# Row sums of the squared queries as plain float32 matmuls, one head per strip of 32 array columns

## What is computed

```python
def rmsnorm(x, g, eps=EPS):
    var = jnp.mean(jnp.square(x), axis=-1, keepdims=True)
    return x * jax.lax.rsqrt(var + eps) * g
...
q = (hidden_states @ Wq).reshape(B, Sq, H, D)      # 16 heads of 128
q = rmsnorm(q, gq)
k = rmsnorm(k, gk)
scores = jnp.einsum('bqhd,bkhd->bhqk', q, k) * scale
attn = jax.nn.softmax(scores, axis=-1)
```

## Time and profile before

| | us |
|---|---|
| median of 3 runs | 1967.53 |
| lowest, highest | 1967.52, 1968.19 |
| span of the profiled execution | 1966.3 |

### The profile page before, as it was taken

The page is one execution under the profiler, slowest core; times in us unless marked ns, Lnnn a source line. Parts: engine busy times, 40 slices in busy tenths (PEclk is TensorE's granted clock), DMA queues, the critical chain, the costliest instruction groups (busy, mean ns, idle before and its releaser), DMA issues.

```text
span 1966.3 us, 33608 instructions
## 1 busy us (share of the span) xinstructions
PE 1946.3 (99%) x11232; PEld 1857.1 (94%) x11232; DVE 1598.0 (81%) x2995; ACT 1008.8 (51%) x2338; POOL 1141.3 (58%) x1272
## 2 busy tenths in 40 slices
PE   8999999999999999999999999999999999999999
PEld 7899899999999999999999999988999999999999
DVE  8878887787887787887778887888888888888875
ACT  5655555555555555555555543444444444444442
POOL 7765655423434333444333335788888888888871
PEclk9999999999999999999999999999999999999999
DMA  6444443423333323233223324211111111111101
GB/s 207 141 127 160 146 151 107 139 92 99 127 109 96 124 101 116 100 119 118 94 91 115 118 94 115 66 33 44 33 33 33 33 33 33 33 33 33 33 1 68
DMA packets 93514, 174.54 MB, mean 89 GB/s; under 512 B 13264, under 2 KB 49760, under 8 KB 91296
## 3 DMA queue, kind: packets, MB, share of 16 engines
q1 hardware_dynamic: 93344, 172.39, 26.7%
HBM read 139.00 MB, written 33.36 MB: 88 GB/s over the span
## 4 chain that ended last, share of the span: by engine, by line
PE 88%; DVE 5%; POOL 3%; issue 2%; ACT 1%; DMA 1%; SPq 0%; DVEq 0%; ACTq 0%; POOLq 0%
PE psum L429 43%; PE psum L819 19%; PE psum L460 6%; PE psum L493 4%; PE psum L516 4%; PE psum L501 4%; PE psum L522 3%; PE psum L517 3%; PE psum L591 1%; PE psum L532 1%; DVE g L1509 0%; DVE ysum L1542 0%; DVE g L1504 0%; DMA xb<-in_x 0%; DVE work L1381 0%
## 5 line engine op out<-in xcount | busy, mean ns | idle before, releaser
L927 ACT ACTIVATE work<-psum,stats,q_rstd 100x361 f32<-100x361 f32 x256 | 163.8, 651 | 166.6 <-DVE stats L1372 166.6
L1271 DVE TENSOR_TENSOR kaT_lo<-psum,kaT_hi 128x488 fp32r<-128x488 f32 (+2 forms) x384 | 213.9, 613 | 41.3 <-ACT kaT_hi L867 41.2
L429 PE MATMUL psum<-wk,ctxT_hi 128*122 128x512 f32 x768 | 241.0, 395 | 0.0
L2043 POOL TENSOR_TENSOR inter_lo<-g,inter_hi 128x400 fp32r<-128x400 f32 x127 | 143.2, 1133 | 125.9 <-ACT inter_hi L867 125.0
L867 ACT CAST kaT_hi<-psum 128x488 fp32r<-128x488 f32 (+2 forms) x384 | 178.7, 540 | 51.7 <-PE psum L501 51.6
L1887 POOL TENSOR_TENSOR k_ss<-k_ss,power 122x4 f32<-122x4 f32 x192 | 194.1, 1011 | 16.0
L1885 POOL TENSOR_SCALAR k_ss<-k_ss 122x4 f32<-122x4 f32 x192 | 37.3, 194 | 260.3 <-DVE k_ss L1327 259.9
L429 PE MATMUL psum<-inter_hi,down_hi 128*128 128x400 f32 x512 | 176.0, 344 | 2.5 <-DVE ysum L1542 1.2
L1362 DVE TENSOR_REDUCE stats<-psum 100x2 f32<-100x722 f32 x128 | 115.7, 904 | 76.2 <-PE psum L460 76.2
L429 PE MATMUL psum<-inter_lo,down_hi 128*128 128x400 f32 x512 | 175.5, 343 | 0.0
L429 PE MATMUL psum<-inter_hi,down_lo 128*128 128x400 f32 x512 | 175.3, 342 | 0.0
(11 more groups left out here) (274 smaller groups left out, 6156.9 us busy)
## 6 DMA issues: line engine op xcount, KB each, us to landing
head_w<-spill_sq SPq DMA_DIRECT2D x48, 512.0 KB, 3.5
head_w<-spill_so SPq DMA_DIRECT2D x46, 512.0 KB, 3.8
wk<-spill_sk SPq DMA_DIRECT2D x12, 1024.0 KB, 4.8
wv<-spill_sv SPq DMA_DIRECT2D x48, 256.0 KB, 2.8
spill_so<-head_w SPq DMA_DIRECT2D x16, 512.0 KB, 3.0
spill_sq<-head_w SPq DMA_DIRECT2D x14, 512.0 KB, 3.0
wk_raw<-in_ctxT SPq DMA_DIRECT2D x12, 361.0 KB, 4.1
spill_sk<-wk SPq DMA_DIRECT2D x4, 1024.0 KB, 6.3
```

Of the source, the lines that this page charges most:

```text
L429: last = e.matmul(out, a_, b_, start=begins and i == 0, stop=ends and i == len(passes) - 1)
L927: e.activation(attn[h][:, 0:SKV], bank[3 + h][0:SQ, 0:SKV], ACT.Exp, bias=st[:, h:h + 1], scale=rq[:, i * QH + h:i * QH + h + 1], accum_ou ...
L1271: e.tensor_tensor(dst, src, high.bitcast(F32), ALU.subtract).then_inc(S[sem], 1)
L2043: e.tensor_tensor(il[:, :], gact[n % 3][:, :], ih[:, :].bitcast(F32), ALU.subtract).then_inc(S["il"], 1)
```

## The change

The squares stay in plain float32 and are not split. Each of the four heads has a buffer `q_sq0` to `q_sq3`; the casts to `q_sqs_hi` on ACT and the subtractions to `q_sqs_lo` on POOL go for quads 1 to 15 and stay for quad 0. `all_squares_summed` makes four plain float32 matmuls with a 128 x 32 matrix of ones (`strip`) as weights. Head h writes partitions 32h to 32h+31 of bank 3, so it uses its own strip of 32 of the array's 128 columns, and each of its 32 partitions holds the same sum. ACT copies all 128 partitions. `sums_transposed` then makes plain float32 matmuls with the 128 x 100 piece of `q_sums` as weights and a 128 x 4 `select` as data, where column h picks partition 32h; before it was a transpose of 4 rows. `strip` and `select` are set up by POOL in the prologue.

```diff
-            q_sq = tensor(a, "q_sq", [P, GT])
-            q_sqs = [pair(a, "q_sqs0", [P, GT])]
+            q_sq = [tensor(a, f"q_sq{h}", [P, GT]) for h in range(QH)]
...
-            select = tensor(a, "select", [P, QH * QH], F32R)
+            select = tensor(a, "select", [P, QH])
+            strip = tensor(a, "strip", [P, STRIP])
...
-            q_sqs += [pair(a, f"q_sqs{h}", [P, GT]) for h in range(1, QH)]
-            q_sums = tensor(a, "q_sums", [QH, GT])
+            q_sums = tensor(a, "q_sums", [P, GT])
...
             def all_squares_summed(quad):
-                e.wait_ge(S["selected"], 2)
+                e.wait_ge(S["selected"], 2 + QH)
+                e.wait_ge(S["qsq"], 4 * quad + QH)
                 for h in range(QH):
-                    e.wait_ge(S["qsh"], 4 * quad + h + 1)
-                    e.wait_ge(S["qsl"], 4 * quad + h + 1)
-                    for k in range(2):
-                        last = e.matmul(bank[3][0:QH, 0:GT], select[:, cols(h, QH)], squares(quad, h)[1][k],
-                                        start=h == 0 and k == 0, stop=h == QH - 1 and k == 1)
+                    last = e.matmul(bank[3][cols(h, STRIP), 0:GT], strip[:, :], squares(quad, h)[0], start=True, stop=True)
                 last.then_inc(S["qsum"], 1)
 
             def sums_transposed(quad):
                 e.wait_ge(S["qsev"], quad)
                 for i in range(GB):
-                    last = e.transpose(bank[7][0:SQ, GT + QH * i:GT + QH * (i + 1)], q_sums[:, cols(i, SQ)], ident[0:QH, 0:QH])
+                    last = e.matmul(bank[7][0:SQ, GT + QH * i:GT + QH * (i + 1)], q_sums[:, cols(i, SQ)], select[:, :], start=True, stop=True)
...
                 e.wait_ge(S["q"], n + 1)
-                if n > QH:
-                    e.wait_ge(S["qsl"], n)
+                if quad > 1:
+                    e.wait_ge(S["qsum"], quad - 1)
                 sq, sqs = squares(quad, h)
                 e.activation(sq, src, ACT.Square).then_inc(S["qsq"], 1)
...
-                hi(sqs[0], sq, "qsh")
+                if quad == 0:
+                    e.wait_ge(S["qsq"], n + 1)
+                    hi(sqs[0], sq, "qsh")
...
-                e.copy(q_sums[:, :], bank[3][0:QH, 0:GT]).then_inc(S["qsev"], 1)
+                e.copy(q_sums[:, :], bank[3][:, 0:GT]).then_inc(S["qsev"], 1)
...
-            e.tensor_scalar(select[:, :], zero[:, :], 1.0, 1.0, ALU.mult, ALU.mult).then_inc(S["selected"], 1)
-            e.wait_ge(S["selected"], 1)
-            e.tensor_scalar(select[:, 0:QH * QH:QH + 1], zero[:, 0:QH], 1.0, 1.0, ALU.mult, ALU.add).then_inc(S["selected"], 1)
+            e.memset(strip[:, :], 1.0).then_inc(S["selected"], 1)
+            e.memset(select[:, :], 0.0).then_inc(S["selected"], 1)
+            e.wait_ge(S["selected"], 2)
+            for h in range(QH):
+                e.tensor_copy(select[:, h:h + 1], ident[:, h * STRIP:h * STRIP + 1]).then_inc(S["selected"], 1)
...
-                if i in (1, 2) and more or u == 3:
-                    query_squares_lo(quad + 1, i - 1)
```

More of the change, by code:

```diff
@@ L57 @@
 WARM = 28
+STRIP = P // QH
 GELU_C = 0.7978845608028654
@@ L396, in squares @@
                 return first_sq[h][:, :], [t[:, :] for t in first_sqs[h]]
-            return q_sq[:, :], [t[:, :] for t in q_sqs[h]]
+            return q_sq[h][:, :], None
         def by_head(i, n):
@@ L1902, in query_squares_lo @@
                 e.wait_ge(S["qsh"], n + 1)
[L1903 to L1906, removed]
                 sq, sqs = squares(quad, h)
@@ L2098, in gpsimd_program @@
                     ln_rstd(1, coming + 2 * (v - 10))
-                if i >= 2 and more and u != 2 and not (i == 2 and late_splits(u)):
-                    query_squares_lo(quad + 1, i)
                 if norm2_at(u) is not None:
@@ L2111, in gpsimd_program @@
                     split_head(n)
-                if i == 2 and u != 2 and late_splits(u):
-                    query_squares_lo(quad + 1, 2)
                 if g + 1 < NG and v == 10 and not late_splits(u):
```

## The result

The changed kernel takes 1964.71 us (median of 20 runs, 1964.1 to 1966.77); the kernel before took 1967.91 us in the same sessions (20 runs, 1967.37 to 1969.28). The ratio is 0.9984 with a 95% interval of 0.9978 to 0.999. It is a little faster, 3.2 us, where 9.9 us slower was forecast. The range given does not hold the time.

The account below looks back on a forecast made before the run. PE's stream was taken as the bound; 15 quads x (0.41 us for the sums of squares + 0.25 for bringing them to rows) gave +9.9 us, 1977.4 us. Its own range was 1972.8 to 1983.3, the 8-in-10 range 1971 to 1995 us.

Parts of the forecast that it names:

- What bounds the kernel: PE's instruction stream sets the time from 90 to 1105 us; relief of ACT and POOL wins at most 1.1 us.
- Term 1, price of a slot: Sums of squares on PE: one plain float32 matmul of 400 columns takes 0.342 us, read from the transposes.
- Term 1, number of slots: Sums of squares: eight strip matmuls, started in program order, take five slots, 1.71 us a quad.
- Term 1, going in and out: Sums of squares: entering and leaving part of the array adds 0.17 us a quad, making the step 1.88 us.
- Term 2: Bringing the sums to rows: eight load and matmul pairs at 0.088 us, +0.25 us a quad, +3.8 us in all.
- The rivals: Sums of squares: strips do not overlap, 1992.8 us, chance 0.28; or all four run together, 1962.0 us, chance 0.15.
- side by side: Sums of squares: all four strips run together in two slots, -5.5 us in all, 1962.0 us; chance 0.15.

Follow-up runs that it names:

- the run with the split left in: Changed kernel, but ACT still casts and POOL still subtracts the squares for all quads and the sums wait for the unused results; 1965.58 us, ratio 0.9987.
- The two orders in float16: Changed kernel with squares split into float16 pairs: both parts head by head, 1960.29 us, or all first parts and then all second parts, 1960.05 us.
- the two strips of 64 columns: Changed kernel with two strips of 64 columns for four of 32, heads 0 and 1 summed in the first, 2 and 3 in the second; 1974.18 us.
- The run on the whole array: The run without strips, with its weights padded to 128 columns so that every matmul uses the whole array; 1985.13 us.
- without strips: Changed kernel's plain float32 unsplit squares, but with 4 weight columns summed in partitions 0 to 3 and sums transposed as before; 1989.43 us, ratio 1.0109.
- the run with the second step in float16: Float16 squares, all first parts first, with the sums also split into float16 by ACT and DVE before being brought to rows; 1964.11 us, ratio 0.998.
- the run with the subtraction ahead of all three: The run with the second step in float16, with DVE's subtraction for the sums' remainder moved ahead of the three key subtractions; 1961.97 us, ratio 0.9966.

## Why the prediction was wrong

*What bounds the kernel*: right. PE idles as little as before, and the run with the split left in shows that ACT's and POOL's relief is worth nothing that the traces can tell (0.1 us of span).

*Term 1, price of a slot*: right. 0.342 us forecast from the transposes, 0.336 measured in line, 0.34 from slot to slot.

*Term 1, number of slots*: the step that failed. The prediction let head 1 start only behind head 0's second matmul. "PE's matmuls start in the order of the program in every row that I read" was true of those rows, but in none of them did a matmul stand behind one that waited for another part of the array. It was a rule about a case that the trace did not contain. The measured number is 2, not 5. Three slots of 0.34 are 1.03 us a quad, 15.4 us in all. The two orders in float16 show that the program's order does not matter here, and the two strips of 64 columns that three waiting matmuls can be passed.

*Term 1, going in and out*: mis-sized. 0.17 forecast, 0.33 measured, +0.16 a quad or 2.4 us. I had read it from transposes of 4 rows: 0.09 before them and 0.08 behind. With the strips it is 0.09 before the first (0.197 in place of 0.104), 0.02 between the two groups, 0.11 before the first L429 (which follows the second group by 0.45 in place of 0.34) and 0.11 before the second L429 (0.288 in place of 0.18). So the way in is as forecast, and the way out costs 0.22 in place of 0.08. The run on the whole array shows the price gone. Together with the slots, term 1 came out at 1.01 us where 1.88 was forecast.

*Term 2*: right. +0.25 forecast, +0.26 measured; eight pairs 0.088 us apart.

*The sum by its own steps with the two corrections*: 9.9 - 15.4 + 2.4 = -3.1 us. Measured: -3.1 in the span and -3.2 in the medians.

*The rivals*: side by side was among them, at 1962.0 us, with a chance of 0.15. It gave the right mechanism and was 2.7 us too low, 2.4 of them by the same 0.16 a quad. Its condition was named rightly, that head 1 starts while head 0's second waits. It was held unlikely on the strength of rows that could not speak to it. With nothing for either end, five and two slots deserved nearer chances, and the range should have reached down to that case.

## What to carry to other kernels

In this kernel the column strips paid. With 32 weight columns for each of four heads, the eight matmuls in plain float32 started in two groups of four, 20 ns within a group and 0.36 us from group to group, so they cost two slots: a step of 1.294 us, against 3.265 for eight in line with 4 columns and 2.980 in line with 128. In float16 eight cost two slots of 0.18 us, in both orders that were tried (0.948 and 0.938 us). The price around the block was 0.33 us in plain float32 and 0.30 and 0.29 in float16. It was paid once for sixteen strip matmuls as for eight (1.966 and 1.294 us), which speaks for having them in one block; no run had them in two blocks a quad. PE is the bound here, and a split into two float16 parts on engines with time to spare (ACT busy for 51% of the span before, POOL for 58%) beat plain float32 on PE: 0.18 against 0.36 us from group to group, 1960.05 against 1964.71 us in all (0.9958 and 0.9984 of the kernel before). Only this case's inputs were run. But a step that makes DVE deliver something new to PE must be placed by DVE's queue in its worst quad, not in its usual one: PE waited 1.5 to 1.6 us for DVE in three quads of 15, and moving one subtraction forward won back 4 us (1964.11 to 1960.12). And when a forecast hangs on a rule such as "in order", ask whether the trace has one case in which the rule could have shown itself broken.

## What the runs showed of the hardware beyond that

- A matmul whose column strip was free started while up to three earlier ones still waited for theirs. In float16 in the order of heads, the hi of heads 1, 2 and 3 have one, two and three of the lo ahead of them in the program and start 7, 13 and 20 ns after the hi of head 0, the first lo 180 ns after it. With two strips of 64 columns the second strip's first matmul has three that wait ahead of it and starts 12 to 14 ns after the first strip's. The starts are 3 or 4 ns apart for neighbours in the program (float16, all first parts first), 6 or 7 for every second one (the changed kernel and float16 in the order of heads), 12 to 14 for every fourth one (two strips of 64 columns).
- The price around a block between matmuls on the whole array is 0.29 us for plain float32 with 4 columns (without strips), 0.33 for strips of 32 in plain float32 (the changed kernel) and 0.30 and 0.29 for them in float16. It is nothing for plain float32 with 128 columns (on the whole array, a step of 2.980 us: the usual 0.104 and 0.183, and eight of 0.336), and nothing for float32r with 4 columns (the kernel before, 1.752 us). It was paid once for a block of eight and once for a block of sixteen (1.294 and 1.966 us).
- Weights of 128 x 100 and 4 columns of data follow each other every 0.088 us in plain float32 (L595 of the changed kernel) and every 0.047 in float16 (L600 of the run with the second step in float16).
- POOL's 60 subtractions of 128 x 400 make DVE 10 us busier (1598.1 us with the split left in, 1587.7 in the changed kernel) with the same 2995 instructions; 9.5 of these us are in the product of two 100 x 2 tensors in SBUF (34.3 against 24.8 us).
- A wait of PE did not always bring the lower clock. In the run with the second step in float16, of three waits of 1.5 to 1.6 us, two were followed by 3.4 us at a granted clock of 0.50 (windows of 5 us with a mean of 0.72 and 0.70), and one was not (1.00). In the first quad a wait of 1.8 us was not followed by it in that run, and waits of 1.4 and 0.4 us were in the run with the subtraction ahead of all three (0.50 from 93.0 to 96.4 us, mean 0.66). The dearest of the three cost 3.3 us for its 1.6.
